# Score matmuls of the first attention layer: two pieces after the transposes, or four pieces between them

## The reference, cut to what matters

```
pre    = silu(x @ Wpre + bpre)
logits = einsum('bnc,bmc->bnm', pre, pre) / sqrt(c)
score  = einsum('bhnd,bhmd->bhnm', q, k) / sqrt(dh)
attn   = softmax(pi[0] * logits[:, None] + score, axis=-1)
out    = einsum('bhnm,bhmd->bhnd', attn, v)
```

## Time and profile before

| | us |
|---|---|
| median of three executions | 1898.95 |
| the profiled execution, its own time | 1901.43 |
| its span, first to last instruction | 1899.7 |
| TensorE matmul busy | 1552.7 (82%) |
| TensorE weight load busy | 1119.6 (59%) |
| VectorE, ScalarE, GpSimd busy | 1053.9, 892.1, 821.5 |

### The profile page before, as it was taken

How to read it: one execution, slowest core, us unless ns; L and a number is a source line. 1 busy time by engine, 2 the same in 40 slices (tenths; PEclk the granted TensorE clock), 3 DMA queues, 4 the chain that set the end, 5 groups by cost and what they waited for, 6 DMA issues and landing times. The chain is left out here.

```text
span 1899.7 us, 46841 instructions
## 1 busy us (share of the span) xinstructions
PE 1552.7 (82%) x16823; PEld 1119.6 (59%) x16823; DVE 1053.9 (55%) x3049; ACT 892.1 (47%) x1558; POOL 821.5 (43%) x1298
## 2 busy tenths in 40 slices
PE   3799999879999993267970589999995899999935
PEld 2476666646766763145650457777774577777734
DVE  5666556476655655732324845666558455566552
ACT  2355455445555551002220367777753566666612
POOL 2266566426665640062450245555541355555500
PEclk9899999999999995588995789999996799999968
DMA  4000000000000000712531056555530555555400
GB/s 120 1 1 2 2 2 2 2 1 1 2 2 2 2 2 5 251 40 54 104 60 32 1 179 185 178 178 178 175 121 1 161 177 179 182 180 177 138 1 22
DMA packets 102762, 147.48 MB, mean 78 GB/s; under 512 B 11632, under 2 KB 59120, under 8 KB 102640
## 3 DMA queue, kind: packets, MB, share of 16 engines
q1 hardware_dynamic: 95856, 140.87, 23.8%
q0 software_dynamic: 6784, 4.87, 1.9%
HBM read 68.49 MB, written 77.21 MB: 77 GB/s over the span
## 5 line engine op out<-in xcount | busy, mean ns | idle before, releaser
L439 DVE CUSTOM_DVE_ANT_0 t_Z<-t_psS,a1b_A 128x1024 f32<-128x1024 f32 x256 | 312.4, 1220 | 202.3 <-issue 202.3
L657 DVE CUSTOM_DVE_ANT_0 t_Z<-t_psS,a0b_L 128x1024 f32<-128x1024 f32 x256 | 311.1, 1220 | 186.3 <-issue 183.0
L715 ACT ACTIVATE t_Pt<-t_psT 128x512 f32<-128x512 f32 x512 | 278.7, 595 | 253.8 <-PE t_psT L613 253.6
L496 ACT ACTIVATE t_Pt<-t_psT 128x512 f32<-128x512 f32 x512 | 278.3, 595 | 191.9 <-PE t_psT L385 191.9
L613 PE MATMUL t_psT<-idf,t_Z 128*128 128x128 f32 x2048 | 285.8, 284 | 8.1 <-issue 6.6
L680 POOL TENSOR_SCALAR t_Z<-t_Z,t_m 128x1024 f32<-128x1024 f32 x256 | 287.3, 1122 | 0.0
L468 POOL TENSOR_SCALAR t_Z<-t_Z,t_m 128x1024 f32<-128x1024 f32 x256 | 286.8, 1120 | 0.0
L385 PE MATMUL t_psT<-idf,t_Z 128*128 128x128 f32 x2048 | 282.0, 281 | 2.0 <-POOL t_Z L468 1.6
L613 PEld LDWEIGHTS t_psT<-idf,t_Z 128*128 128x128 f32 x2048 | 226.6, 144 | 59.4 <-issue 32.1
L385 PEld LDWEIGHTS t_psT<-idf,t_Z 128*128 128x128 f32 x2048 | 227.7, 144 | 42.5 <-issue 37.4
L467 POOL TENSOR_TENSOR t_touch<-t_m 128x1 f32<-128x1 f32 x256 | 49.4, 193 | 270.1 <-DVE t_m L439 268.2
(11 more groups left out here) (252 smaller groups left out, 1766.9 us busy)
## 6 DMA issues: line engine op xcount, KB each, us to landing
relative_rows<-t_rows SPq DMA_DIRECT2D x256, 256.0 KB, 2.0
a1b_A<-relative_rows SPq DMA_DIRECT2D x192, 192.0 KB, 2.5
a1b_A<-relative_rows SPq DMA_DIRECT2D x64, 128.0 KB, 2.3
x_B<-in_b SPq DMA_DIRECT2D x1, 4096.0 KB, 19.3
x_A<-in_a SPq DMA_DIRECT2D x1, 4096.0 KB, 26.7
expert_rows<-zp SPq DMA_DIRECT2D x1, 2740.0 KB, 12.7
x_xe<-expert_rows SPq DMA_DIRECT2D x8, 342.5 KB, 2.9
x_WP<-in_moe_pre SPq DMA_DIRECT2D x8, 256.0 KB, 3.4
```

The costliest lines, as they stand in the source:

```text
L439: nc.vector.tensor_tensor_reduce(out=Z[:, qt % 2, :], in0=psS[:], in1=A[:, qt, :], scale=1.0, scalar=3e38, op0=ALU.add, op1=ALU.min, accum ...
L496: nc.scalar.activation(Pt[:, qt % 2, half * (N // 2):(half + 1) * (N // 2)], psT[:, half, :], ACT.Exp).then_inc(s_exp, 1)
L657: nc.vector.tensor_tensor_reduce(out=Z[:, j, :], in0=psS[:, j % 2, :], in1=L[:, qt, :], scale=1.0, scalar=3e38, op0=ALU.add, op1=ALU.min, ...
L715: nc.scalar.activation(Pt[:, qt % 2, j, half * (N // 2):(half + 1) * (N // 2)], psT[:, half, :], ACT.Exp).then_inc(s_exp, 1)
```

## The change

The four 256-column pieces of a tile's scores are issued between the transposes: with T for a transpose and S for a score piece, TensorE's order becomes T S T T S T, T S T T S T (the comma is the border between the halves of psT), then the values. The wait for s_z stands before the first piece. The last piece raises s_s, as the second matmul did.

```diff
-                def scores(hq, i, v):
+                def scores(hq, i, v, part):
                     qt, j = i // J, i % J
-                    if not (type(v) is int and v < 2):
+                    if part == 0 and not (type(v) is int and v < 2):
 
                         pe.wait_ge(s_z, v - 1)
-                    for k0 in (0, 512):
-                        last = nc.tensor.matmul(psS[:, j % 2, k0:k0 + 512], QT[0:KR, hq * J + j, qt * P:(qt + 1) * P],
-                                                KT[0:KR, hq * J + j, k0:k0 + 512], start=True, stop=True)
-                    last.then_inc(s_s, 1)
+                    k0 = part * 256
+                    last = nc.tensor.matmul(psS[:, j % 2, k0:k0 + 256], QT[0:KR, hq * J + j, qt * P:(qt + 1) * P],
+                                            KT[0:KR, hq * J + j, k0:k0 + 256], start=True, stop=True)
+                    if part == 3:
+                        last.then_inc(s_s, 1)
...
                             for k in range(4):
                                 kt = half * 4 + k
                                 last = nc.tensor.transpose(psT[:, half, k * P:(k + 1) * P], Z[:, j, kt * P:(kt + 1) * P], idf[:])
-                            last.then_inc(s_t, 1)
-                        if i + 3 < NTILE:
-                            scores(hq, i + 3, u + 3)
-                        elif not final:
-                            scores(hq + 1, i + 3 - NTILE, u + 3)
+                                if k == 3:
+                                    last.then_inc(s_t, 1)
+                                if k % 2 == 0:
+                                    if i + 3 < NTILE:
+                                        scores(hq, i + 3, u + 3, kt // 2)
+                                    elif not final:
+                                        scores(hq + 1, i + 3 - NTILE, u + 3, kt // 2)
...
                 for i in range(3):
-                    scores(0, i, i)
+                    for part in range(4):
+                        scores(0, i, i, part)
```

## The result

The changed kernel takes 1906.32 us in the median of five executions (1905.64 to 1911.17) against 1899.23 us for the kernel before in the same comparison (1897.33 to 1901.57). The ratio is 1.0044, 95% interval 1.0027 to 1.006: slower by 0.44%. Forecast were 1907.0 and slower. The profiled execution took 1911.17 us, the slowest of the five.

A forecast was written before the change was run, and what follows sets the result against it. TensorE's start-to-start steps per tile were taken as the bound: +31 ns x 230 tiles = +7.1 us, plus 1.0 us at divisions, gives +8.1 us, a median of 1907.0 us; range 1898.5 to 1913.

The forecast's parts named there:

- TensorE's pitches are the bound, and the array stays full: Steady tile: the sum of TensorE's start-to-start steps, 2.03 us before, sets the time; TensorE stays busy throughout at full clock.
- The bare piece: One 256-column score matmul on TensorE, without switch costs: 0.109 us, four 0.436 against 0.433 now, so +3 ns per tile.
- A score after a transpose, +4 ns: Each score piece following a transpose on TensorE costs 4 ns more; four per tile, 16 ns, one already in the 0.433.
- rival A: Switching between transposes and scores is free: +3 ns per tile, 0.7 us, with divisions 0.7 to 2.8, about 1900.7; chance 0.28.
- A transpose after a score, +3 ns: Each return from a score piece to a transpose on TensorE costs 3 ns (bounds 0 and 9), four per tile, 12 ns.
- The sum: TensorE per steady tile: 436 + 16 + 12 = 464 ns against 433, +31 ns; over 230 tiles +7.1 us.
- The divisions: Tiles after a division, where VectorE is late for the earlier s_z wait: 14 x 0.07 = +1.0 us, at most 2.1.
- The sequencer costs nothing: TensorE's sequencer: two more matmul and load pairs per tile and their register instructions add nothing, since it runs ahead.
- The covers: Steady tile: ScalarE's second exponential, 0.46 us later, keeps 0.5 us and more spare; VectorE and GpSimd get slack, so no cost.
- change of kind: On TensorE, switching between transposes and score pieces, priced at 4 ns one way and 3 ns the other.

The follow-up runs named there:

- the kernel with the split alone: Kernel before with four 256-column score pieces instead of two of 512, all still behind the eight transposes; tile 2.0355 us, ratio 1.0025 (1.0014 to 1.0036).
- the kernel with the scores first: Kernel before with the two 512-column score matmuls and their wait for s_z moved ahead of the tile's eight transposes; tile 1.987 us, ratio 0.9954 (0.9941 to 0.9966).

## Why the prediction was right

- *TensorE's pitches are the bound, and the array stays full*: right, in every kernel with the old place of the values.
- *The bare piece*: 0.109 taken, 0.108 to 0.109 in the kernel with the split alone, which costs 4.5 ns per tile against my 3.
- *A score after a transpose, +4 ns*: 112 to 113 ns against 109 in the trace after, four times. Right, and so rival A is out.
- *A transpose after a score, +3 ns*: 111 to 112 against 109, but only three times; the last transpose hands over to the values at the old 203 ns. I had counted four.
- *The sum*: +31 ns a tile forecast, +22 measured. The rest of the difference is that the step from a transpose to a score is 108 where I had 109. 230 x 22 ns = 5.1 us instead of 7.1.
- *The divisions*: +1.0 us forecast. In the trace the score after a division comes 0.165 to 0.174 after T0, so at most 0.01 x 14 = 0.1 us. My own working gave 206.51 against 206.50, 0.01; the 0.07 was a choice inside bounds whose upper one, 0.15, assumed that issuing a load behind the wait costs as much again. That failed, and so did the 0.06 for the score's load: it was an f32 transpose's, and a bf16 score's is short, as the kernel with the scores first showed.
- *The sequencer costs nothing*: wrong at four tiles, the one after each reload of Vh in the loop body. There T0 itself has waited, the sequencer has no lead, and its register instructions stand between T0 and S0: 0.21 instead of 0.165, 0.2 us in all. In the last quad, which has no such instructions, the step at that place is 0.164. The tile with the reload itself, which I had left out, is 2.145 us where it was 2.142 (a tile of a loop quad), so leaving it out was right.
- *The covers* (ScalarE's later second half, VectorE, GpSimd): held, no new wait in the steady tile.
- *The cause* of the switch I hadn't named beyond "change of kind". It is the change in the number of rows.

So +8.1 was a sum of terms right in kind, two of them too large, while 2 to 3 of the measured us aren't in any term (the intervals would allow none): the nearness of 1907.0 to 1906.32 is partly luck.

## What to carry to other kernels

Where the matmul row has no gap, count the steps from start to start, by which instruction follows which: the dear ones are passages between shapes that use the array differently. Interleaving two kinds of matmuls gains nothing when both are held by their stream, and adds a few ns per change of rows; putting like with like gains, most of all for matmuls with narrow weights (16 in a row to 64: -1.6%). And let the matmul with the shortest weight load follow such a passage. When a matmul is moved forward, its wait moves too: look at the few tiles where the engine that it waits for is late, since there it holds up everything queued behind it.

## What the runs showed of the hardware

- An f32 transpose of 128 columns and a bf16 matmul of 256 take the same 109 ns of the array at full granted clock, and the f32 weight load hides under as little as 55 to 60 ns.
- Going from 128 rows to 72 or 96 and back costs about 3 to 4 ns and 3 ns; at 128 rows throughout nothing that the steps of 109 to 110 ns show.
- The first matmul behind the values pays 56 ns for an f32 load, some 6 for a bf16 one.
- Executions of one kernel differ by up to 9 us, and stretches with identical code had granted clocks from 0.82 to 1.00.
